# Gated cross attention with a top-1 mixture of experts: scale and shift of the second norm stored with each row, and another order around the sort

## What is computed

```python
x = x + tanh(g_xattn) * cross_attention(layernorm(x), ctx)     # scores unscaled, softmax / sqrt(256)
xn = layernorm(x)                                              # (x - mean) * rs = rs * x + shift
e = argmax(xn @ router_w.T)                                    # one expert for each token
for e in range(8):                                             # 704 inner features
    y[tokens of e] = (silu(xe @ gate_w[e].T) * (xe @ up_w[e].T)) @ down_w[e].T
x = x + tanh(g_ffn) * y
```

## Time and profile before

| | |
|---|---|
| median of 3 runs | 231.97 us (230.15, 231.97, 232.58) |
| profiled execution, own time | 228.05 us |
| its span, first to last instruction | 226.0 us |
| PE, busy share of the span | 89% |
| DVE, ACT, POOL | 58%, 49%, 60% |
| mean granted TensorE clock | 0.965 of full speed |

### The profile page before, as it was taken

How to read it: one execution, slowest core, us unless ns; L and a number is a source line. 1 busy time by engine, 2 the same in 40 slices (tenths; PEclk the granted TensorE clock), 3 DMA queues, 4 the chain that set the end, 5 groups by cost and what they waited for, 6 DMA issues and landing times.

```text
span 226.0 us, 4507 instructions
## 1 busy us (share of the span) xinstructions
PE 200.3 (89%) x1194; PEld 170.4 (75%) x1194; DVE 131.7 (58%) x434; ACT 109.7 (49%) x223; POOL 136.6 (60%) x138
## 2 busy tenths in 40 slices
PE   5998999997666789999999999999999999999630
PEld 2766899886566578888877888888888888888520
DVE  2689699957799055446526556636546546555410
ACT  2448777764410552764375674375674442244100
POOL 3001379496484996199849989849989952231110
PEclk9999999999887999999999999999999999999975
DMA  6999214928500229512920670941030021210000
GB/s 222 312 392 390 93 50 122 362 100 279 213 0 23 73 80 361 188 48 64 381 70 2 229 256 1 355 135 35 4 92 1 25 73 26 51 46 4 28 19 3
DMA packets 11541, 29.42 MB, mean 130 GB/s; under 512 B 1938, under 2 KB 7957, under 8 KB 10486
## 3 DMA queue, kind: packets, MB, share of 16 engines
q1 hardware_dynamic: 6576, 20.46, 25.4%
q0 software_dynamic: 2064, 5.12, 7.6%
q10 hardware_dynamic: 2870, 3.48, 4.6%
HBM read 24.85 MB, written 4.72 MB: 131 GB/s over the span
## 4 chain that ended last, share of the span: by engine, by line
PE 65%; issue 9%; DMA 6%; DVE 6%; POOL 5%; ACT 3%; SPq 1%; ACTq 0%; POOLq 0%
PE ps L916 32%; PE ps L928 12%; PE ps L895 5%; PE ps L931 5%; DMA xin<-in_x 4%; POOL wgu L416 3%; DMA both<-in_WdL 3%; PE ps L795 2%; PE ps L775 2%; PE ps L888 2%; POOL wd L420 2%; PE ps L764 2%; DVE st L989 1%; PE ps L816 1%; PE ps L755 1%
## 5 line engine op out<-in xcount | busy, mean ns | idle before, releaser
L916 PE MATMUL ps<-wgu,xhT 128*128 x360 | 81.5, 379 | 1.3 <-issue 1.3
L916 PEld LDWEIGHTS ps<-wgu,xhT 128*128 128x128 f32 x360 | 65.2, 188 | 12.0 <-issue 1.5
L928 PE MATMUL ps<-wd,hT 128*128 x120 | 44.2, 404 | 2.6 <-DVE hT L1174 2.6
L461 POOL DMA_INDIRECT xin<-x_rows,table x23 | 22.7, 985 | 28.7 <-DVE xin L1195 22.1
L393 POOL TENSOR_TENSOR wgu<-raw_gu,wgu (+1 forms) x12 | 38.6, 3251 | 0.1
L1182 DVE TENSOR_TENSOR A<-xin,ps 128x512 f32<-128x512 f32 (+1 forms) x40 | 20.4, 519 | 28.2 <-ACT xin L655 14.7
L655 ACT ACTIVATE xin<-ps 128x512 f32<-128x512 f32 (+1 forms) x40 | 18.2, 465 | 32.5 <-PE ps L916 32.4
L466 POOL DMA_INDIRECT out<-xin,table x20 | 20.3, 1015 | 21.0 <-DVE xin L1195 15.8
L928 PEld LDWEIGHTS ps<-wd,hT 128*128 128x128 f32 x120 | 23.0, 192 | 7.8 <-issue 3.5
L931 PE MATMUL ps<-wd,hT 128*128 x100 | 28.5, 285 | 0.0
L649 ACT ACTIVATE hT<-ps 128x512 fp32r<-128x512 f32 x20 | 11.8, 592 | 32.0 <-PE ps L895 32.0
(11 more groups left out here) (156 smaller groups left out, 304.6 us busy)
## 6 DMA issues: line engine op xcount, KB each, us to landing
raw_gu<-in_Wgu SPq DMA_DIRECT2D x8, 1408.0 KB, 7.9
both<-in_Wd SPq DMA_DIRECT2D x8, 640.0 KB, 4.8
xin<-in_x SPq DMA_DIRECT2D x8, 256.0 KB, 8.6
x_rows<-x ACTq DMA_DIRECT2D x8, 256.0 KB, 4.2
both<-in_WdL SPq DMA_DIRECT2D x16, 64.0 KB, 5.2
both<-in_ctxT ACTq DMA_DIRECT2D x1, 960.0 KB, 6.9
xin<-x_rows,table POOLq DMA_INDIRECT x23
out<-xin,table POOLq DMA_INDIRECT x20
```

The costliest lines, as they stand in the source:

```text
L461: pool.indirect_dma_start(out=xg[:, j % SEATS, :], out_offset=None, in_=rows, in_offset=bass.IndirectOffsetOnAxis(ap=table[:, j:j + 1], ax ...
L916: last = pe.matmul(ps[:, g, 0:2 * WIDE if g < 2 else 4 * REST], xhT[:, j % 2, x_part, c, :], w, start=(c == 0 and (x_part, w_part) == (0, 0)),
L928: last = pe.matmul(ps[:, 6, 0:2 * H], hT[:, 0, c, :], wd[:, slot, c].rearrange("p o a n -> p (o a n)"), start=(c == 0), stop=(c == CI - 1) ...
```

## The change

- **Rows.** `x1_rows` has 258 floats a token: x1, scale and shift. x1 is written over x in `xin`, whose rows are 258 wide; POOL's `newton` writes scale and shift into their last two columns. The room `x1`, the three bf16 parts, `rsel`, the 16 matmuls at L878 and `stat` go; ACT reads scale and shift from the seat of the gathered row.
- **Writing the rows.** Instead of eight DMAs of one batch on ACT's queue there are two: tiles 0 to 5 (`FIRST`) by ACT in its round 6, tiles 6 to 15 (`LATER`) by SP at e = 2, after the loads of expert 2's down weights and before `arrived_d(2)`. Each waits for its scales. `newton` runs twice on POOL, for `FIRST` between `low_pieces(0)` and `low_pieces(1)`, for `LATER` after both; DVE makes a guess for `FIRST` in round 3.
- **Last batch.** PE turns x1 of batch 7 before the logits of batch 6; the last logits go to bank 6, the last turned x1 to another room, so neither waits for its predecessor's reader. On DVE the guess for `LATER` comes ahead of route(6) and route(7).
- **Sort.** Counts are rounded by adding and subtracting 2^23 in three operations instead of four and a memset. The high mask and its first product come first; DVE makes 11 low masks, ACT five (Square of the distance, then Relu of one minus that) and the second product; POOL makes none. PE takes the low masks as they come. The adding up of `past` is one reduction, `turn` one operation less.
- **Spin.** 36 and 40 matmuls instead of 64 and 24.

The core of the diff:

```diff
-SHARE = 3
+SHARE = 5
+FIRST, LATER = slice(0, 3 * TB), slice(3 * TB, NTOK)
...
-        rows = nc.dram_tensor("x1_rows", (N + 1, H), F32, kind="Internal").ap()
+        rows = nc.dram_tensor("x1_rows", (N + 1, HR), F32, kind="Internal").ap()
...
+                if e == SPLIT - 1:
+                    sp.wait_ge(p_st2, 2)
+                    sp.dma_start(rn[:, LATER], xin[:, LATER, :]).then_inc(d_row, 16)
                 arrived_d(e)
...
-            for e in range(SPLIT - 1):
-                low_pieces(e)
-
-            pool.wait_ge(v_guess, 1)
-            link(newton(pool, link, mv2[:, :, 0], rs2[:, 0, :], rs2[:, 1, :], ALL))
...
-            pool.wait_ge(v_slot, 1)
-            for t in range(NTOK - SHARE, NTOK):
-                ins = pool.tensor_scalar(ohlo[:, t, :], iota_lo[:], slot_f[:, 0, t:t + 1], None, ALU.is_equal)
-            ins.then_inc(p_lo, 1)
...
+            low_pieces(0)
+            scales2(FIRST, 1)
+            low_pieces(1)
+            scales2(LATER, 2)
+
+            pool.wait_ge(d_row, 32)
             pool.wait_ge(d_zrow, 16)
             pool.wait_ge(v_tab, 1)
...
+                if i == B - 2:
+                    act.wait_ge(p_st2, 1)
+                    act.dma_start(rn[:, FIRST], xin[:, FIRST, :]).then_inc(d_row, 16)
...
+            act.wait_ge(v_slot, 1)
+            for t in range(SHARE):
+                ins = act.activation(far[:, t, :], iota_lo[:], ACT.Square, scale=-1.0, bias=slot_f[:, 0, t:t + 1])
+            ins.then_inc(a_far, 1)
+            act.wait_ge(a_far, 1)
+            act.activation(ohlo[:, 0:SHARE, :], far[:], ACT.Relu, scale=-1.0, bias=one[:, 0:1]).then_inc(a_lo, 1)
+            act.wait_ge(v_hi, 1)
+            act.activation(uv[:, :, 1, :], ohhi[:], ACT.Copy, scale=iota_p[:, 0:1]).then_inc(a_uv, 1)
...
-                               scale=stat[:, 0, j:j + 1], bias=stat[:, 1, j:j + 1]).then_inc(a_xh, 1)
+                               scale=scale_of(j), bias=shift_of(j)).then_inc(a_xh, 1)
...
-            spin(64)
-            pe.wait_ge(v_lo, 1)
-            pe.wait_ge(p_lo, 1)
-            for t in range(NTOK):
+            spin(36)
+            pe.wait_ge(v_uv, 1)
+            pe.wait_ge(a_uv, 1)
+            for n, t in enumerate(list(range(SHARE, NTOK)) + list(range(SHARE))):
+                if t >= SHARE:
+                    pe.wait_ge(v_lo, t - SHARE + 1)
+                else:
+                    pe.wait_ge(a_lo, 1)
...
-                last = pe.matmul(ps[:, 3, 0:6 * NT], ohlo[:, t, :], rsel[:, t].rearrange("p a n -> p (a n)"), start=(t == 0), stop=(t == NTOK - 1))
-            last.then_inc(t_stat, 1)
-
-            spin(24)
+            spin(40)
...
-            dve.wait_ge(p_r3, 1)
-            weighed(0)
...
             dve.tensor_copy(table[:], tab2[:]).then_inc(v_tab, 1)
-            weighed(1)
```

More of the change, by code:

```diff
@@ L152, in part @@
             return view, start + size
-        quiet = x1[:, 0, 0, :].bitcast(BF16)
+        quiet = V[:, 0, :].bitcast(BF16)
         free_c = both[:, 0:C * B * K]
@@ L159, in flamingo_moe @@
         uv, _ = part(free_c[:, at:at + NTOK * NT].bitcast(BF16), 0, NTOK, 2, NT)
-        rsel, _ = part(V[:].rearrange("p b h -> p (b h)")[:, 0:NTOK * 3 * NT].bitcast(BF16), 0, NTOK, 6, NT)
+        far, _ = part(V[:].rearrange("p b h -> p (b h)").bitcast(BF16), 0, SHARE, P)
         mean_w = V[:, B - 1, 0:P]
@@ L168, in flamingo_moe @@
         rk, at = part(free_q, at, NTOK, E)
-        xg, at = part(free_x, 0, SEATS, H)
+        xg, at = part(free_x, 0, SEATS, HR)
         og, at = part(free_x, at, RING, H)
@@ L211, in flamingo_moe @@
         p_chain = sem("p_chain")
-        v_guess, p_r3 = sem("v_guess"), sem("p_r3")
-        v_slot, p_lo = sem("v_slot"), sem("p_lo")
-        v_rsel, t_stat, v_stat = sem("v_rsel"), sem("t_stat"), sem("v_stat")
+        v_guess, p_st2 = sem("v_guess"), sem("p_st2")
+        v_slot, v_hi, a_far, a_lo, a_uv, v_uv = sem("v_slot"), sem("v_hi"), sem("a_far"), sem("a_lo"), sem("a_uv"), sem("v_uv")
         v_sort = sem("v_sort")
@@ L308, in _ @@
             xv = x.rearrange("b (t p) h -> b p t h", p=P)
+            rn = rows[0:N].rearrange("(n p) h -> p n h", p=P)
             for b in range(B):
@@ L369, in _ @@
                 lambda: pool.memset(mean_w, 1.0 / H),
+                lambda: pool.memset(one[:], 1.0),
             ]
@@ L1087, in _ @@
                     context(i + 1)
+                if TB * i == FIRST.stop:
+                    dve.wait_ge(v_aggr, i)
+                    guess(dve, link, mv2[:, FIRST, 1], FIRST).then_inc(v_guess, 1)
             dve.wait_ge(v_aggr, B)
-            guess(dve, link, mv2[:, :, 1], ALL).then_inc(v_guess, 1)
+            guess(dve, link, mv2[:, LATER, 1], LATER).then_inc(v_guess, 1)
+            route(B - 2)
             route(B - 1)
```

138 lines of the change are left out of this document (56 added, 82 removed).

## The result

The changed kernel takes 231.99 us (median of 4 runs, 231.6 to 233.25) beside 231.06 for the kernel before in the same job (4 runs, 227.63 to 232.58). The ratio is 1.0162, 95% interval 1.0104 to 1.022: slower, where 229.1 and faster was forecast. The forecast's range ended at 231.7. The ratio leaves out executions over 1.5% above the fastest of their kernel, which is why it shows 1.6% where the two medians show 0.4%. Four executions of each don't give the size of the loss more closely, and the changed kernel was not run again in the later jobs.

A forecast was written before the change was run, and what follows sets the result against it. PE bounds the kernel from the first expert tile on, whose start waits for the sort's table and first gather. Table 2.1 plus gather 0.8 gives 2.9 us off 231.97: 229.1, range 227.3 to 231.7.

The forecast's parts named there:

- what costs nothing: Side effects taken as free, among them DVE's three extra operations in round 3, 0.6 us, in slack against PE.
- `newton` for the first batches: On POOL before the low pieces: 4.4 us where 2.86 was idle, so later POOL work comes 1.55 us later, without cost.
- The gather: First gather after the table: 1.04 us too long, read as POOL held up by DVE; 0.8 us to be gained.
- First tile at the low clock: Rival: the first expert tile's 18 matmuls run at 1.2 GHz, 1.5 us lost, 230.6; chance 0.07.
- the last batch's order: End of attention: turning batch 7 before the logits of batch 6 gains 0.9 us.
- the counts: Sort: three linked operations instead of four and a memset, 0.6 us instead of 0.95, 0.35 gained.
- ACT's chain: Sort masks: five Squares 1.6 us, Relu 0.85, product about 0.6, sum 3.05 with the link; last of the three chains.
- the products at the low clock: PE's 16 products for the table may run at 1.2 GHz and take 1.15 us instead of 0.57.
- The rows issued as one write: `LATER` rows, 1.32 MB issued at 61.3, land at 66.6, 1.0 us before the table, hidden with little cover.
- the rival's price: Rival, gather unchanged: the 1.04 us is the price of any first gather, products at the low clock, 230.3; chance 0.15.
- the second rival: Rows late: rows land at 68.5 or ACT's split is 1.2 us late, table's lead lost, 230.1; chance 0.15.
- the rival for slower: Write of many odd-length rows at a third of the rate, 110 GB/s, landing 74.6: 3.9 us slower, 235.9; chance 0.05.

The follow-up runs named there:

- g3_before: Kernel before plus only the three early guess operations for tiles 0 to 5 on DVE at the end of round 3: 232.39 us, ratio 1.0125.
- a_psum: Changed kernel with the round 3 guess passing through PSUM bank 6 in four operations, one step earlier: 228.13 us, ratio 0.9944.
- a_g4: Changed kernel with the guess of tiles 0 to 5 one round later: 233.41 us, ratio 1.0181.
- c_spin: Kernel before with 36 and 40 fillers on PE instead of 64 and 24: 229.37 us, ratio 1.0045.
- c_one: Changed kernel with the early group undone: one guess and one `newton` at the end, all rows written then: 229.12 us, ratio 1.0033.
- c_masks: b_place with ACT's last split of expert 2's down weights behind its masks: 227.02 us, ratio 0.9961.
- c_start: b_place with seven instead of five fillers at the very start: 226.76 us, ratio 0.9927.
- b_start: b_all with seven instead of five filler matmuls ahead of the first projection: 227.84 us, ratio 0.9939.
- b_place: b_all with the first `newton` behind both low pieces and all row writes on SP's queue: 226.84 us, ratio 0.9848.
- b_all: Changed kernel with the guess through PSUM and 64 and 64 fillers instead of 36 and 40: 229.17 us.
- b_warm: b_all with one early indirect gather that nobody reads, on POOL before the second `newton`: 230.15 us.

## Why the prediction was wrong

**The step that failed** is in the part on what costs nothing: "DVE's three extra operations in round 3 (0.6 us) lie in slack that DVE has against PE". They were priced at what they take alone, 0.2 each. They took 3.11 us, since each waited for an operation of POOL, and the slack was less than that; after PE's wait of 2.26 its clock was at the lower level, and x1 came 3.14 us later than with the detour. g3_before shows that these operations alone do it, a_psum that the detour, in a place one step earlier, undoes it. The sign was in before's own trace, in rows that I didn't read. DVE's L979, an operation of the same kind from SBUF to SBUF, in pairs:

```profile
30.14 1.42 DVE L979 TENSOR_SCALAR xn<-xin,rs,nm 128x255 f32<-128x255 f32 x2
...
36.87 3.74 POOL L420 TENSOR_TENSOR wd<-both,wd 128x512 fp32r<-128x512 f32 x3
...
39.43 1.65 DVE L979 TENSOR_SCALAR xn<-xin,rs,nm 128x255 f32<-128x255 f32 x2
```

A pair takes 0.73 at 21.95, beside POOL operations of 0.2 us, and 0.72 at 25.42, where POOL is idle, but 1.34 to 1.65 beside the low pieces (1.24 us and 0.9 each). I had asked what DVE does to POOL at the gather, and not for each DVE operation what POOL does at that moment.

In the profiled executions 2.9 us less was forecast and 3.8 more measured, 6.7 apart: 4.10 in the attention, 1.70 at the start, 0.72 at the gather and 0.19 in the sort. The 1.70 are chance. And the base of 229.1 was high by chance as well: 231.97 was the median of three runs, and before's medians in the later jobs were 229.13 to 230.02.

**`newton` for the first batches**, "4.4 us where POOL was idle for 2.86", was thought hidden. In after it was, behind the stall. The delay was smaller than worked out (L429 at 44.62 in a_psum, 1.15 later than 43.47, not 1.55), but without the stall ACT waits for the weights, and that cost 0.67. Where the guess is later it costs as much as the stall did (a_g4).

**The gather.** I took 0.8 of 1.04 and got 0.08. The long DVE operation is gone and the first gather still starts 0.95 behind the table and takes 1.22; it takes 1.18 with DVE idle. So POOL was not held up by DVE in the way that I read; the good fit in time was chance. The long operation is worth 0.13 us of the gather's length: 1.34 and 1.35 beside it (before, g3_before, c_spin), 1.21 and 1.22 without it. The rest is nearly the rival's price, though not one of any first gather: with a table that has long been ready the gap is 0.29 (c_one, c_masks).

**First tile at the low clock** had a chance of 0.07 and a price of 1.5. It happened in this execution and took 2.15 more; before's execution, however, lost about as much at later tiles (first tile to last turn 134.25, where c_spin with the same code there and a fast first tile has 132.03), so by chance it doesn't show in the difference. The clock is at 0.50 at 80 to 84 in after.

**Right, in size too:** the last batch's order, 0.86 of 0.9 (x1 to `oh` 3.84 instead of 4.70); the counts, 0.31 of 0.35, though 0.28 went again on PE's side, whose clock was low there (`oh` to the first count 1.39 instead of 1.11); ACT's chain, 1.57 + 0.83 + 0.59 for 3.05 with its links (partly luck: a line through rows 6 and 7 gives an operation a fixed part of 0.42, not 0.3, but the five Squares in a row follow each other by 0.31); the products at the low clock (0.77, between 0.57 and 1.15); sum 1.91 of 2.1. What PE waited for last was DVE's low masks (72.09), not ACT's product (72.06), so the two chains came out equal. The rows issued as one write took 6.4 us instead of 5.3 (why, no run shows):

```profile
x_rows<-xin SPq DMA_DIRECT2D x1, 1290.0 KB, 6.4
```

They landed near 73.1, half a microsecond before the table; c_one and c_masks show that this cover is as thin as the second rival had it. A write as slow as the rival for slower had it did not occur: the 1290 KB landed 6.0 to 8.1 us after their issue in the eleven kernels that write them, and 2 MB 9.0 us after the first issue (c_one). None of my rivals had the attention in it at all; I had bounded the change by the part that it was about.

## What to carry to other kernels

Price an added VectorE operation by what GpSimd does at that moment, not by its own length: beside GpSimd's long operations a 128x6 `tensor_scalar` within SBUF took up to 1.2 us instead of 0.17, and by way of PSUM each operation took 0.16 or 0.17. In a pipeline near its limit a stall can be paid twice, once as the wait and once as TensorE's clock after it. And when an engine's idle time is filled, ask what it frees for others by being early: moving `newton` behind the low pieces gave 0.67 us in the attention. In the totals that gain isn't shown: c_start has 0.9927 and b_start, without the move, 0.9939, and between x1 and the table c_start takes 13.29 where b_start takes 12.48. With the detour, the move and more fillers the kernel is faster than before by about 1% (b_place, ratio 0.9848; c_start, 0.9927).

## What the runs showed of the hardware

The times of one kernel spread over almost 3% (before: 226.95 to 233.28 in one job), and they go with PE's clock: its mean over an execution was 0.956 to 0.965 below 228 us and 0.936 to 0.950 above 231. PE's waits of 1.84 us in c_start, 1.58 in b_all and 2.26 in after were followed by a granted clock of 0.50 for 2 us and more, but a_psum's, 1.57 us within 52 to 54, was not; once, in b_all, the clock stayed there for 12 us though PE was mostly busy. At the start of after the eight score-weight matmuls took 4.90 us instead of 3.49 while the windows showed 1.00, so a duration can tell more than that column. The first gather starts 0.93 to 0.95 us behind the table where the rows landed early, and 0.29 behind the rows where the table had been ready for 1.3 us and more (c_one, c_masks); the two together give every start that was seen but b_warm's (0.81 behind the table). Whether the 0.95 comes of a fresh table or of DVE's small operations that run beside it stays open. And an execution that is earlier at one point need not end earlier: c_start's 0.8 us at 9 us (beside b_place) became a longer wait, a dip, and 1.8 us lost at 30.
